# Zero rows on GpSimd's DMA queue, and ScalarE's work for a later half in four blocks: a recurrence with a mixture of experts on one core

## The chip, the cores and the metric

The kernel runs on one core of a Trainium2 chip. The metric is the time of one execution on the device in microseconds. Five engines with their own instruction queues work beside one another and meet at semaphores: TensorE (PE, matmuls and transposes), VectorE (DVE), ScalarE (ACT), GpSimd (POOL) and SyncE (SP), which here only issues transfers. Sixteen DMA engines do the moving.

## The reference, cut to what matters

The input x has 4 sequences of 1024 tokens with 256 channels. It is normalised over the channels to xn, and xn goes two ways.

- A recurrence over the 1024 time steps: for every sequence and channel a state of 16 numbers, `h = dA_t * h + dB_t * x_t`. The decay is `dA = exp(clamp(dt * A))` with `dt = clamp(softplus(xn @ Wdt.T + b))`, and `B = xn @ WB.T`, `C = xn @ WC.T`. After each step the state of each sequence is scaled down to a norm of 20 where it is above, so step t needs the norm of step t-1. The output of a step is `y = sum_n h * C + Dp * x`.
- A mixture of 8 experts with top 2 of 8 and 1280 slots each: every token is sent to its two experts' slots, each expert does `gelu(x @ c_fc) @ c_proj` on its slots, and the results come back with their weights.

The output is `x + s * silu(experts)`, where s is the recurrence's output.

## The kernel before

**Preparation.** Eight chunks of 128 tokens by 4 sequences are loaded, normalised by VectorE (`statistics`, `normalize`, lines 583 to 607), turned by TensorE (`turn`, line 1039) and evacuated by ScalarE (`turned`, line 803). SyncE stores each chunk three times: as rows (`xnd`, line 361), times Dp (`dx`, line 363) and turned (`xts`, line 366). Line 606 makes `dx` in one of two buffers, so it waits for the store two chunks earlier. Then VectorE works out the slot of each token (lines 671 to 711), and its first step follows.

**The zero rows.** The slots of the experts that get no token have to hold zeros. `clear(i)` writes 1024 of the 10240 rows of `xg`, 1 KB each, from a tile of zeros (lines 354 to 356). Eight of the ten stand in SyncE's queue ahead of the eight chunks' stores, two behind them. GpSimd scatters the tokens onto `xg` later (`send`, line 507), two steps apart from step 12 on, and before its first scatter it waits for all ten (line 545).

**The recurrence.** VectorE does 1024 steps, each with six operations (lines 722 to 755); GpSimd gives each step's scale (line 531) between lines 725 and 751. TensorE and ScalarE make what the steps need, four steps (a quad) at a time: TensorE transposes the decays (line 1176) and spreads the inputs with `pick` (line 1182), ScalarE copies the first to `da` (line 959) and scales the second to `ur` (line 966). Sixteen steps are a block, four blocks (64 steps) a half. VectorE waits for a quad's `ur` at line 736. ScalarE may be at most about two blocks ahead (line 946), TensorE waits for ScalarE's `ur` of the quad before (line 1178).

**Work for later halves.** For a half h, ahead of its time:
- TensorE's `time_rates(h, 6)` (line 1062) and ScalarE's `logs_of(h, 6)`: four copies out of PSUM (lines 817, 819), Exp (823) and Ln (824); then VectorE's `add_all_logs` (618) and ScalarE's `soft_clamp` (828).
- TensorE's `b_and_c` (1072) and ScalarE's `b_and_c_out` (836 to 838).
- ScalarE's `squares_of` (844), TensorE's `sums_of_squares` (1082, 1084) and ScalarE's `sums_out` (850).
- ScalarE's decays of the next half: 32 Tanh operations, two or three a quad (line 858), and at the end of a group of four blocks four exponentials over the whole half (`decay_ops`, line 870). TensorE waits for these before the next group's first transposes (line 1167).

All of the TensorE parts use PSUM bank 6, which the experts' row turns (line 1118) use as well; the tuple `waiting` names the last eviction of it that has to be done. Before, ScalarE does `logs_of` at the end of each group's fourth block, directly behind `decay_ops`; TensorE's `time_rates` is behind the fourth block's fourth quad.

**The experts' work** lies between the quads in a list fixed when the kernel is built: `by_quad` gives each quad up to three items, "up" (line 1194, eight matmuls, then a Gelu on ScalarE, line 974), "turn" (line 1118, then a copy, line 978) and "down" (line 1210, 16 matmuls a time, then a copy, line 985). It begins at quad 39, after all the scatters.

**ScalarE's functions** need a table each; where the next function isn't in the loaded ones, an ACT_TABLE_LOAD stands in the trace ahead of it.

Of the kernel before, what the change touches and what calls it, by code (L numbers as in the profile page):

```python
# [18 lines left out]
NB, NT, D, NS = 4, 1024, 256, 16  # L19
NE, CAP, FF = 8, 1280, 1024  # L20
P = 128
# [3 lines left out]
CH = NT // P  # L25
# [3 lines left out]
NBLK = NT // BLK  # L29
# [4 lines left out]
SLOTS = NE * CAP  # L34
# [10 lines left out]
HALVES = NT // HALF  # L45
# [6 lines left out]
def build(nc, x, wdtT, bdt, wb, wc, a_log, dpar, w_g, c_fc, c_proj, out):  # L52
# [4 lines left out]
    with ctx:  # L57
# [20 lines left out]
        zeros = sb("zeros", [P, 2 * D])  # L78
# [247 lines left out]
        delayed = sorted(k + 1 for k in at_step)  # L326
        sum_at, input_at, norm_at = {}, {}, {}
        for h in range(2, HALVES):
            for table, pieces, lo_, hi_ in ((sum_at, 1, 4 * h - 8, 4 * h - 6), (input_at, 2, 4 * h - 5, 4 * h - 3), (norm_at, 1, 4 * h - 2, 4 * h)):
                lo_, hi_ = max(lo_ * BLK + 3, BLK + 2), max(hi_ * BLK, 2 * BLK)  # L330
                free_ = [k for k in delayed if lo_ <= k < hi_ and k not in sum_at and k not in input_at and k not in norm_at]
                spare = [k for k in range(lo_, hi_) if k not in free_ and k not in sum_at and k not in input_at and k not in norm_at]
                chosen = sorted((free_ + spare)[:pieces])
                assert len(chosen) == pieces, (h, lo_, hi_)
                for c, k in enumerate(chosen):
                    table[k] = (h, c)
# [5 lines left out]
        def _(sp):  # L342
# [8 lines left out]
            for b in range(NB):  # L351
                sp.dma_start(dx[0:YPAD, b, :], zeros[0:YPAD, 0:D]).then_inc(padz, 16)

            def clear(i):
                sp.dma_start(xg[i * NT:(i + 1) * NT, :].rearrange("(r p) d -> p r d", p=P),
                             zeros[:, 0:D].unsqueeze(1).broadcast_to([P, CH, D])).then_inc(moe_zero, 16)

            for i in range(CH):
                clear(i)
                sp.wait_ge(xn_ready, i + 1)  # L360
                sp.dma_start(xnd.rearrange("(b i p) d -> p b i d", p=P, i=CH)[:, :, i, :], xnat[:, :, i, :]).then_inc(xn_out, 16)
                sp.wait_ge(dxn_ready, i + 1)
                sp.dma_start(dx_tok[:, i], dxn[:, i % 2]).then_inc(dx_done[i % 2], 16)
                if i >= 1:
                    sp.wait_ge(xt_sb, i + 1)
                    sp.dma_start(xts[i], xnT[:, i]).then_inc(xT_out, 16)
# [11 lines left out]
            sp.wait_ge(padz, 16 * (NB + 1))  # L378
            sp.sem_inc(y_out, 1)
            sp.dma_start(dxt, dx[0:BLK, :, :].rearrange("t b (k d) -> (t b k) d", k=DH)).then_inc(dx_in, 16)  # L380
            for i in range(CH, SLOTS // NT):
                clear(i)
            for k in range(2):
                sp.wait_ge(dx_done[k], 16 * CH // 2)
            sp.wait_ge(xn_out, 16 * CH)
# [74 lines left out]
        def _(pool):  # L460
# [42 lines left out]
            for i in range(CH):  # L503
                pool.wait_ge(stat_ready, i + 1)
                g.tensor_tensor(rs[:, :, i], vare[:, i, :], neghalf[:, :], ALU.pow).then_inc(rstd_ready, 1)

            def send(n):

                j, k = divmod(n, 2)
                first, home = homes[home_of(j)]  # L510
                g.indirect_dma_start(out=xg, out_offset=bass.IndirectOffsetOnAxis(ap=slot_of[:, k, j:j + 1], axis=0),  # L511
                                     in_=home[:, j - first, :], in_offset=None).then_inc(sent, 16)
# [27 lines left out]
            for step in range(NT):  # L540

                kind, n = at_step.get(step, ("", 0))
                if kind == "send":
                    if n == 0:
                        pool.wait_ge(moe_zero, 16 * (SLOTS // NT))
                    else:
                        pool.wait_ge(sent, 16 * n)
# [233 lines left out]
        def _(act):  # L781
# [161 lines left out]
            for blk in range(NBLK):  # L943
# [7 lines left out]
                for q in range(QPB):  # L951
# [38 lines left out]
                        weights_of(quad - COMBINE_AT)  # L990
                    if 0 <= quad - COMBINE_AT - 1 < 2 * CH:
                        gate_of(quad - COMBINE_AT - 1)
                    if blk % 4 == 0 and blk > 0 and q == 1 and blk // 4 + 2 < HALVES:
                        b_and_c_out(blk // 4 + 2, 6)
                    if blk % 4 == 1 and q == 0 and 2 <= blk // 4 + 1 < HALVES:
                        sums_out(blk // 4 + 1, 6)
                    if q == QPB - 1 and blk + 1 < NBLK:
                        inputs_out_of_psum(blk + 1)
# [14 lines left out]
                        decay_ops(1 - f).then_inc(decay_ready, 1)  # L1013
                    if q == 2 and blk < 3:
                        decay_op(0, blk + 1)
                    if blk == 0 and q == 1:
                        logs_of(2, 6)
                    if blk == 0 and q == 2:
                        b_and_c_out(2, 6)
                if blk % 4 == 3 and blk + 4 < NBLK:  # L1020
                    if (blk + 9) // 4 < HALVES:
                        logs_of((blk + 9) // 4, 6)
                if blk % 4 == 2 and blk // 4 + 2 < HALVES:
                    soft_clamp(blk // 4 + 2)
                if blk % 4 == 0 and 2 <= blk // 4 + 1 < HALVES:
                    squares_of(blk // 4 + 1)
            act.wait_ge(u_done, QUADS + 1)
            act.sem_inc(u_done, 1)
# [6 lines left out]
        def _(pe):  # L1035
# [126 lines left out]
            for blk in range(NBLK):  # L1162
# [5 lines left out]
                for q in range(QPB):  # L1168
# [43 lines left out]
                            last.then_inc(mm2_ps, 1)  # L1212
                    if 0 <= quad - COMBINE_AT < 2 * CH:
                        combine(quad - COMBINE_AT)
                    h = {(3, 3): blk // 4 + 3, (0, 1): blk // 4 + 2, (1, 0): blk // 4 + 1}.get((blk % 4, q), 0)
                    if blk == 0:
                        h = {1: 2, 2: 2}.get(q, 0)
                    if 2 <= h < HALVES:
                        if turns:
                            pe.wait_ge(xt_in, turns)  # L1220
                        after_evictions()
                        if blk % 4 == 3 or (blk == 0 and q == 1):
                            pe.wait_ge(xch_in[h // 2 % 2], 16 * ((h // 2 + 1) // 2))
                            time_rates(h, 6)
                            waiting = [z_used, h + 1]
                        elif blk % 4 == 0:
                            b_and_c(h, 6)
                            waiting = [bc_used, h + 1]
                        else:
# [48 lines left out]
```

## Time and profile before

| | |
|---|---|
| median of 3 runs | 1704.61 us (1703.8 to 1704.99) |
| the profiled execution | 1704.6 us, span 1702.6 us |
| VectorE busy | 1549.6 us (91%) |
| TensorE busy | 1291.1 us (76%), weight loads 1136.9 (67%) |
| ScalarE busy | 1225.1 us (72%) |
| GpSimd busy | 770.4 us (45%) |
| DMA | 113.29 MB, 67 GB/s in the mean; 332 and 340 GB/s in the first two fortieths |

The span falls into four stages: preparation (0 to 80 us), steps with the scatters beside them (to about 326), steps with the experts' matmuls (to about 1500), steps with the gathers and the end. Times in the rows are from the span's start. A row of waits names the instruction that waited, what released it, the sum in us, how often and the longest. Idle time before an instruction stands in brackets at the end of a row of the timeline, with what ended it. The engines' names in the rows are PE, ACT, DVE, POOL and SP; "q" behind one is its instruction queue.

### The profile page before, as it was taken

To read this page: it belongs to the slowest core of one execution; us is meant where nothing else is said; L and a number is where in the kernel's file an instruction comes from. 1 tells how busy PE (TensorE), PEld (TensorE's weight loads), DVE (VectorE), ACT (ScalarE), POOL (GpSimd) and SP (SyncE) were. 2 spreads that over 40 slices of the span, in tenths; PEclk is the share of its full clock that TensorE was granted. 3 is DMA by queue.
4 is the path that set the end of the run, shared out by engine and by line. 5 is a ranking of instruction groups with operands and counts; after the bars stand their busy time and mean duration, and the time that the engine had idled before them with its cause. 6 is when DMAs were issued, how large, how long until landed. Compare 5 with 4: busy or idle time off the path is not lost.

```text
span 1702.6 us, 33871 instructions
## 1 busy us (share of the span) xinstructions
PE 1291.1 (76%) x9356; PEld 1136.9 (67%) x9356; DVE 1549.6 (91%) x9454; ACT 1225.1 (72%) x3152; POOL 770.4 (45%) x1254
## 2 busy tenths in 40 slices
PE   5864435297979797997979798897979798855661
PEld 5753324286868686886868687796878687744551
DVE  6688888899999999998999899999989999987778
ACT  3697548278787887868787887878787777756451
POOL 3156666543434344343444344343434434468842
PEclk8576767698989899998989999898989899877785
DMA  9931111210111021021002002011101110012245
GB/s 332 340 127 47 44 41 44 95 36 17 51 49 46 17 77 31 18 62 50 28 24 86 24 26 75 25 39 37 63 18 34 66 32 20 20 44 71 75 127 202
DMA packets 95533, 113.29 MB, mean 67 GB/s; under 512 B 8432, under 2 KB 85360, under 8 KB 95344
## 3 DMA queue, kind: packets, MB, share of 16 engines
q1 hardware_dynamic: 87696, 94.13, 17.0%
q0 software_dynamic: 6144, 16.79, 3.1%
q8 instruction: 74, 1.21, 0.3%
q14 instruction: 115, 0.94, 0.2%
q10 hardware_dynamic: 1504, 0.22, 0.1%
HBM read 60.91 MB, written 50.20 MB: 65 GB/s over the span
## 4 chain that ended last, share of the span: by engine, by line
PE 54%; DVE 14%; ACT 12%; issue 7%; POOL 7%; DMA 4%; SPq 1%; POOLq 0%; ACTq 0%; DVEq 0%
PE ps L1210 15%; PE ps L1194 13%; PE ps L1182 10%; PE ps L1176 6%; ACT arena L870 4%; POOL arena L531 4%; DVE arena L751 3%; POOL xg L511 3%; PE ps L1141 3%; PE ps L1157 3%; DVE arena L722 2%; DVE arena L728 2%; DVE arena L740 2%; DVE arena L736 2%; ACT arena L858 2%
## 5 line engine op out<-in xcount | busy, mean ns | idle before, releaser
L531 POOL TENSOR_TENSOR arena<-arena,neghalf 128x1 f32<-128x1 f32 x1025 | 591.8, 577 | 851.2 <-DVE arena L725 780.3
L751 DVE SCALAR_TENSOR_TENSOR arena<-arena 128x128 f32<-128x128 f32 x1024 | 361.6, 353 | 54.0 <-POOL arena L531 53.6
L1182 PE MATMUL ps<-arena,pick 128*128 128x128 f32 x2048 | 301.9, 294 | 38.8 <-ACT arena L966 19.8
L736 DVE CUSTOM_DVE_ANT_0 arena<-arena 128x128 f32<-128x128 f32 x1024 | 294.0, 287 | 30.3 <-ACT arena L966 25.4
L1176 PE MATMUL ps<-ident,arena 128*128 128x128 f32 x1024 | 210.7, 333 | 137.6 <-ACT arena L870 132.0
L966 ACT ACTIVATE arena<-ps,arena 128x128 f32<-128x128 f32 x1024 | 291.4, 376 | 32.8 <-PE ps L1182 32.8
L1182 PEld LDWEIGHTS ps<-arena,pick 128*128 128x128 f32 x2048 | 280.2, 211 | 50.9 <-ACT arena L966 38.0
L1194 PE MATMUL ps<-arena,wf 128*128 128x256 f32 x1280 | 302.0, 386 | 8.1 <-issue 8.1
L728 DVE CUSTOM_DVE_ANT_0 arena<-arena 128x128 f32<-128x128 f32 x1024 | 299.0, 292 | 0.0
L1210 PE MATMUL ps<-wp,arena 128*128 128x256 f32 x1280 | 295.8, 385 | 2.6 <-ACT arena L974 2.3
L1176 PEld LDWEIGHTS ps<-ident,arena 128*128 128x128 f32 x1024 | 179.9, 244 | 167.4 <-ACT arena L870 137.2
L722 DVE TENSOR_TENSOR arena<-arena 128x128 f32<-128x128 f32 x1024 | 290.3, 283 | 0.0
L740 DVE TRANSPOSE_TENSOR_REDUCE arena<-arena 128x2 f32<-128x64 f32 x1024 | 251.3, 245 | 35.5
L858 ACT ACTIVATE arena<-arena,a16c,a 128x256 f32<-128x256 f32 x512 | 278.7, 610 | 0.1
L1194 PEld LDWEIGHTS ps<-arena,wf 128*128 128x128 f32 x1280 | 240.7, 195 | 38.9 <-issue 9.3
L1210 PEld LDWEIGHTS ps<-wp,arena 128*128 128x128 f32 x1280 | 241.7, 194 | 34.1 <-ACT arena L974 2.7
L755 DVE TENSOR_TENSOR_SCAN arena<-arena 128x2 f32<-128x2 f32 x1024 | 220.7, 215 | 0.0
L959 ACT ACTIVATE arena<-ps 128x512 f32<-128x512 f32 x256 | 151.9, 593 | 74.4 <-PE ps L1176 74.0
L725 DVE TENSOR_SCALAR arena<-arena 128x1 f32<-128x1 f32 x1024 | 149.3, 146 | 0.0
L974 ACT ACTIVATE arena<-ps 128x512 f32<-128x512 f32 x160 | 95.3, 607 | 62.5 <-PE ps L1194 59.9
L920 ACT ACTIVATE arena<-arena,winmask 128x16 f32<-128x16 f32 x520 | 110.9, 316 | 21.2 <-POOL arena L538 21.0
L1137 PE MATMUL ps<-arena,ident 128*128 128x128 f32 x132 | 32.6, 334 | 109.8 <-ACT arena L920 105.5
(146 smaller groups left out, 1379.7 us busy)
## 6 DMA issues: line engine op xcount, KB each, us to landing
xg<-zeros SPq DMA_DIRECT2D x10, 1024.0 KB, 9.6
xrow<-xg SPq DMA_DIRECT2D x40, 256.0 KB, 2.7
yg<-arena SPq DMA_DIRECT2D x40, 256.0 KB, 2.2
arena<-in_x SPq DMA_DIRECT2D x16, 512.0 KB, 9.3
wf<-in_c_fc SPq DMA_DIRECT2D x8, 1024.0 KB, 5.0
wp<-in_c_proj SPq DMA_DIRECT2D x8, 1024.0 KB, 6.0
arena<-dx SPq DMA_DIRECT2D x66, 64.0 KB, 2.4
ys<-arena SPq DMA_DIRECT2D x66, 64.0 KB
```

Source lines behind the costliest of these rows:

```text
L531: g.tensor_tensor(sv[:, slot, 1:2], mx, neghalf[:, 0:1], ALU.pow).then_inc(s_ready, 1)
L722: v.tensor_tensor(vv, hr[:, before, :], da[:, slot, :], ALU.mult).then_inc(v_ready, 1)
L728: v.tensor_tensor_reduce(out=junk[:, 0, :], in0=vv, in1=ur[:, slot, :], scale=2.0 / CLAMP ** 2, scalar=0.0, op0=ALU.mult, op1=ALU.add, acc ...
L736: v.tensor_tensor_reduce(out=junk[:, 1, :], in0=vv, in1=vv, scale=1.0 / CLAMP ** 2, scalar=0.0, op0=ALU.mult, op1=ALU.add, accum_out=ac[:, ...
L740: v.tensor_reduce(out=terms[:, slot, 0:2], in_=ac.unsqueeze(2).broadcast_to([P, 2, 32]), axis=AX.X, op=ALU.add, apply_transpose=True).then ...
L751: v.scalar_tensor_tensor(hr[:, slot, :], vv, sv[:, before, 1:2], ur[:, slot, :], ALU.mult, ALU.add)\
L858: last = a.activation(dst[:, :, k, n_, :], src[:, :, k, :], ACT.Tanh, scale=a16[:, c:c + 1], bias=a16c[:, c:c + 1])
L966: last = a.activation(ur[:, t + j, :], ps[2][:, j * P:(j + 1) * P], ACT.Copy, scale=terms[:, t + j, 3:4])
L1176: last = t.transpose(ps[q % 2][:, j * P:(j + 1) * P], tanhb[:, f, :, s], ident[:, :])
L1182: last = t.matmul(ps[2][:, j * P:(j + 1) * P], pick[:, q * QUAD + j, :], xin, start=True, stop=True)
L1194: last = t.matmul(ps[4 + j % 2][:, c * TS:(c + 1) * TS], wf[:, k, (2 * j + c) * P:(2 * j + c + 1) * P], xt[:, k, :], start=k == 0, stop=k ...
L1210: last = t.matmul(ps[7][:, j * D:(j + 1) * D], hid[:, k, j * P:(j + 1) * P], wp[:, k, :], start=k == 0, stop=k == FC - 1)
```

## The change

The ten transfers of zeros are issued by GpSimd, behind its last `rstd` and ahead of the clearing of `sv`, `hr` and `win`. Before its first scatter GpSimd also waits for `memz`. For halves from 2 on, `time_rates` and `logs_of` stand in the second quad of a group's first block, `b_and_c` and its copies in the second quad of the second block, `sums_of_squares` and its copy in the first quad of the third, `squares_of` at the end of the second. VectorE's `add_all_logs` comes 16 steps later (`sum_at`). `soft_clamp` and `decay_ops` stay.

```diff
-            for table, pieces, lo_, hi_ in ((sum_at, 1, 4 * h - 8, 4 * h - 6), (input_at, 2, 4 * h - 5, 4 * h - 3), (norm_at, 1, 4 * h - 2, 4 * h)):
+            for table, pieces, lo_, hi_ in ((sum_at, 1, 4 * h - 7, 4 * h - 5), (input_at, 2, 4 * h - 5, 4 * h - 3), (norm_at, 1, 4 * h - 2, 4 * h)):
...
-            def clear(i):
-                sp.dma_start(xg[i * NT:(i + 1) * NT, :].rearrange("(r p) d -> p r d", p=P),
-                             zeros[:, 0:D].unsqueeze(1).broadcast_to([P, CH, D])).then_inc(moe_zero, 16)
-
             for i in range(CH):
-                clear(i)
                 sp.wait_ge(xn_ready, i + 1)
...
-            for i in range(CH, SLOTS // NT):
-                clear(i)
...
+            for i in range(SLOTS // NT):
+                g.dma_start(xg[i * NT:(i + 1) * NT, :].rearrange("(r p) d -> p r d", p=P),
+                            zeros[:, 0:D].unsqueeze(1).broadcast_to([P, CH, D])).then_inc(moe_zero, 16)
+
             def send(n):
...
                     if n == 0:
+                        pool.wait_ge(memz, 1)
                         pool.wait_ge(moe_zero, 16 * (SLOTS // NT))
...
-                    if blk % 4 == 0 and blk > 0 and q == 1 and blk // 4 + 2 < HALVES:
+                    if blk % 4 == 1 and q == 1 and blk // 4 + 2 < HALVES:
                         b_and_c_out(blk // 4 + 2, 6)
-                    if blk % 4 == 1 and q == 0 and 2 <= blk // 4 + 1 < HALVES:
+                    if blk % 4 == 2 and q == 0 and 2 <= blk // 4 + 1 < HALVES:
                         sums_out(blk // 4 + 1, 6)
...
-                    if blk == 0 and q == 1:
-                        logs_of(2, 6)
-                    if blk == 0 and q == 2:
-                        b_and_c_out(2, 6)
-                if blk % 4 == 3 and blk + 4 < NBLK:
-                    if (blk + 9) // 4 < HALVES:
-                        logs_of((blk + 9) // 4, 6)
+                    if blk % 4 == 0 and q == 1 and blk // 4 + 2 < HALVES:
+                        logs_of(blk // 4 + 2, 6)
                 if blk % 4 == 2 and blk // 4 + 2 < HALVES:
                     soft_clamp(blk // 4 + 2)
-                if blk % 4 == 0 and 2 <= blk // 4 + 1 < HALVES:
+                if blk % 4 == 1 and 2 <= blk // 4 + 1 < HALVES:
                     squares_of(blk // 4 + 1)
...
-                    h = {(3, 3): blk // 4 + 3, (0, 1): blk // 4 + 2, (1, 0): blk // 4 + 1}.get((blk % 4, q), 0)
-                    if blk == 0:
-                        h = {1: 2, 2: 2}.get(q, 0)
+                    h = {(0, 1): blk // 4 + 2, (1, 1): blk // 4 + 2, (2, 0): blk // 4 + 1}.get((blk % 4, q), 0)
...
-                        if blk % 4 == 3 or (blk == 0 and q == 1):
+                        if blk % 4 == 0:
...
-                        elif blk % 4 == 0:
+                        elif blk % 4 == 1:
```

## Rows read from the trace of the kernel before

**Rows 1.** Page, costliest groups: operation, count, busy us, mean ns, idle before, releaser.
```profile
L736 DVE CUSTOM_DVE_ANT_0 arena<-arena 128x128 f32<-128x128 f32 x1024 | 294.0, 287 | 30.3 <-ACT arena L966 25.4
```

**Rows 2.** Busy us by engine (PE, PEld, DVE, ACT, POOL), granted clock, DMA, middle stage.
```profile
397.40:1450.40 1053.00, 923.97 (x6784) 820.64 (x6782) 1006.36 (x6362) 841.17 (x2144) 416.97 (x746) 0.95 0.13 41
```

**Rows 3.** Waits in the middle stage: VectorE's, TensorE's and ScalarE's longest.
```profile
DVE arena L736 <- ACT arena L966: 21.7, 10, 3.8
...
PE ps L1176 <- ACT arena L870: 89.9, 10, 9.0
...
ACT arena L985 <- PE ps L1210: 61.4, 27, 2.3
```

**Rows 4.** The same view as rows 2: the first and the last of eleven groups.
```profile
397.40:493.05 95.65, 85.73 (x627) 76.31 (x626) 92.96 (x590) 77.07 (x197) 38.63 (x69) 0.95 0.15 48
...
1360.69:1450.44 89.75, 79.03 (x600) 70.05 (x598) 86.30 (x546) 72.28 (x190) 35.68 (x64) 0.97 0.08 25
```

**Rows 5.** Timeline of TensorE around one group's decays (start us, us, operation, count).
```profile
671.18 1.91 PE L1062 MATMUL ps<-arena 128*128 128x256 f32 x8
...
682.19 1.15 PE L1176 MATMUL ps<-ident,arena 128*128 128x128 f32 x4 [8.99 <-ACT arena L870]
...
695.23 0.85 PE L1176 MATMUL ps<-ident,arena 128*128 128x128 f32 x4
695.92 1.06 PE L1182 MATMUL ps<-arena,pick 128*128 128x128 f32 x8
696.81 1.89 PE L1194 MATMUL ps<-arena,wf 128*128 128x256 f32 x8
698.54 0.60 PE L1118 MATMUL ps<-ident,xrow 128*128 128x128 f32 x4
```

**Rows 6.** Timeline of ScalarE around the same decays.
```profile
673.23 0.28 ACT L912 ACTIVATE arena<-ps 128x128 f32<-128x128 f32 x1 [1.25 <-PE ps L1124]
673.53 1.28 ACT L870 ACT_TABLE_LOAD   x1
...
682.04 0.46 ACT L817 ACTIVATE arena<-ps,arena 128x256 f32<-128x256 f32 x1
...
683.61 0.63 ACT L823 ACTIVATE arena<-arena 128x512 f32<-128x512 f32 x1
684.26 1.28 ACT L824 ACT_TABLE_LOAD   x1
685.56 0.63 ACT L824 ACTIVATE arena<-arena 128x512 f32<-128x512 f32 x1
...
686.21 1.70 ACT L920 ACTIVATE arena<-arena,winmask 128x16 f32<-128x16 f32 x8
687.80 0.57 ACT L959 ACTIVATE arena<-ps 128x512 f32<-128x512 f32 x1
688.27 1.11 ACT L966 ACTIVATE arena<-ps,arena 128x128 f32<-128x128 f32 x4
689.40 1.28 ACT L974 ACT_TABLE_LOAD   x1
```

**Rows 7.** The same view as rows 2: preparation and the steps before the first scatter.
```profile
0.00:72.00 72.00, 49.30 (x313) 45.50 (x314) 46.27 (x150) 40.67 (x79) 22.68 (x36) 0.70 1.01 345
72.00:98.00 26.00, 18.22 (x132) 14.95 (x131) 23.40 (x120) 17.90 (x43) 7.22 (x13) 0.63 0.87 282
```

**Rows 8.** Timeline of VectorE in the preparation.
```profile
25.76 1.23 DVE L606 TENSOR_TENSOR wf<-arena 128x1024 f32<-128x1024 f32 x1 [3.22 <-DMA dx<-wf]
...
65.35 0.42 DVE L675 COPY arena<-ps 128x256 f32<-128x256 f32 x1 [4.82 <-PE ps L1054]
```

**Rows 9.** Timeline of GpSimd: the first scale and the first scatter.
```profile
80.94 0.59 POOL L531 TENSOR_TENSOR arena<-arena,neghalf 128x1 f32<-128x1 f32 x1 [26.29 <-DVE arena L725]
...
99.99 1.24 POOL L511 DMA_INDIRECT xg<-wf,slot_of  x1 [0.23 <-issue]
```

**Rows 10.** The zero rows' issues on SyncE: duration in ns, min/median/max.
```profile
L355 SPq DMA_DIRECT2D xg<-zeros x10: 434/1233/1668, 15.7 to 75.7; - x10
```

## The prediction

> **What bounds the kernel now.** I read the page's costliest groups first. VectorE carries the recurrence, 1024 steps of six operations, and hardly ever stops: in the whole run 25.4 us stand before line 736, where it waits for ScalarE's `ur` [rows 1]. The edits of ScalarE's order can win these at most. Next I cut the span by stage. In the middle stage (397 to 1450 us: eleven groups of 64 steps, the expert matmuls beside them) VectorE is busy 1006 of 1053 us, TensorE 924, ScalarE 841 [rows 2]. Busy shares don't say who leads, so I read the waits of that stretch. TensorE waits 89.9 us for the decay exponentials (line 870), about 9.0 in each group. ScalarE waits for TensorE; its longest row is 61.4 us, and no row of it in this stretch names VectorE. VectorE waits 21.7 us for ScalarE [rows 3]. So TensorE and ScalarE run freely at TensorE's pace and VectorE catches up with them once per group. A group takes 95.65 us (first of eleven) to 89.75 us (last), 95.7 in the mean, (1450.44 - 397.40) / 11 [rows 4]. TensorE's ledger for these 1053 us is 924 of work, 90 at the decays and the rest small. VectorE alone would need (1053 - 21.7) / 11 = 93.8. What makes TensorE's order longer makes the kernel longer, one for one; what shortens it pays only down to 93.8, about 21 us in all.
>
> **ScalarE's lump, taken apart.** Before, ScalarE runs the four decay exponentials at the end of a group's fourth block and the logs of a later half directly behind them. TensorE has the half's time-rate matmuls behind it by then: 8 matmuls of 1.9 us before it stops for 8.99 us [rows 5]. The logs fall beside TensorE's first matmuls of the next group: from 682.19 on, that engine shows no wait, although ScalarE makes the four evacuations, Exp, a table load and Ln from 682.04 to 686.1 [rows 5, 6]. They are covered.
> The change moves the time rates and the logs to the second quad of the next group's first block, and B and C, the sums and the squares by one block each. What follows:
> - At the decays the 1.9 us of time rates go, so the last transpose comes earlier, and with it the copy of line 912, which waited 1.25 us for it here [rows 6]. The decays start 1.3 us earlier in this group, up to 2 in others, and TensorE's stop of 9.0 stays, since it is the decays' own length.
> - The same 1.9 us now stand among TensorE's other work. Together: 0 to +0.6 us per group.
> - The logs lose their cover. I walk the group after the lump at 682, where the third quad holds one "up" (8 matmuls) and a "turn", and the fourth a "down". After the time rates TensorE has left, until it needs ScalarE's next `ur` (the picks of the fourth quad): four transposes 0.69, eight picks 0.89, the up 1.73, the turn 0.5, four transposes 0.69, in all 4.5 us (start to start) [rows 5]. ScalarE in that time: four evacuations 1.57, a table load 1.28, Exp 0.65, a load 1.30, Ln 0.63, then `da` 0.47 and `ur` 1.11 of the third quad, 7.0 us [rows 6]. TensorE stops for 2.5. Then ScalarE needs another load (1.28) and 0.6 for the Gelu that the down waits for, while TensorE has 0.9 of picks: another 1.0. Cost here 3.5 us.
> - The load before Exp is new. After a Gelu the resident tables lack Exp (a load stands before the decays too, at 673.53 [rows 6]), and now a Gelu mostly comes between decays and logs. Where the logs stood right behind the decays, Exp follows with no load [rows 6].
> - Gained: the window copies (from 686.21) come earlier and TensorE's output matmuls no longer wait for them, 0.5 us a group at most.
> I walked both engines' orders through all eleven groups with these durations. For the order before this gives 95.9 us per group (the trace: 95.7), for the new order 99.2: between -0.5 and +4.9 by group, because a group whose first quads hold only "down" keeps its tables and has more to do. Eleven groups: +36. Without the new load before Exp the same walk gives 2.2 per group, +25; with all table loads at nothing, +10; below, where TensorE could always fill the gap, the 21 us that VectorE waits could go. I take +31, between the first two, because the loads' row is plain and their number is not. Once, 2 us come back: `ur` of a group's first quad is 5 us earlier, but VectorE then meets the third quad's, which is later. Lump: +29.
> The row for tables is the load of 1.28 us that stands before the first Gelu after Ln [rows 6]. The Trainium skill (ScalarE: Activation LUTs, "Table sets: the hidden batching unit") speaks against this move: calls are to be batched by table set, not by function, and the logs' Exp and the decays' Exp were such a batch. By its figure of 2.7 us for a switch, two more a group would be 59 us of ScalarE; by the row they are 28, and only what TensorE cannot fill counts.
> The soft clamp's and the norms' waits stay met: ScalarE is at most two blocks ahead, and VectorE's additions for a half, now 16 steps later, are still more than a block before their readers. No cost.
>
> **The zero rows.** Ten transfers of 1 MB (1024 rows of 1 KB each) leave SyncE's queue, where issuing one took 1.23 us in the median [rows 10]. What goes is their share of the transfers beside the preparation: in 0 to 72 us the DMA engines are full (share 1.01, 345 GB/s) [rows 7]. VectorE waits there for the stores of `dx`, 3.22 us at 25.76 being the first of five. But the routing, which leads to the first step, starts at 65.35 after 4.82 us of waiting for TensorE's logits [rows 8]; so only part of a faster VectorE arrives. Bounds 0 and 8; I take 2, as ScalarE's logs and TensorE's queue of logits stand right behind the first of these waits.
> What comes: ten issues in GpSimd's queue before it clears `hr`, `sv` and `win`, and VectorE's first step waits for that. GpSimd stands idle for 26.3 us before its first scale at 80.94 [rows 9], so the issues are hidden up to 2.6 us each. The trace has no such issue. Nearest rows: the same transfer on SyncE, 1.23 us, and GpSimd's scatter of 128 rows, 1.24 us [rows 9, 10]. If the price goes by rows it is 8 x 1.24 = 9.9 us. The same regular transfer is the nearer row, as the scatter must read an index for each row; I take up to 2.5, so nothing, and keep 9.9 for the range.
> The clears must land before the first scatter. Before, 72 x 345 + 26 x 282 GB/s = 32 MB were moved by 98 us [rows 7], just before the first scatter at 99.99 [rows 9]. Now the first 50 us hold only loads and stores, 4.5 MB of inputs and zeros and six chunks of 1.57 MB, so 14 MB. The other 18 MB need 53 us at 345 GB/s and end at 103. The scatter's turn would be at 98. If the row loads end last, no wait; if the clears do, 5 us. I take 3. Zero rows together: -2 + 3 = +1, from -8 to +5.
> The DMA engines were full whoever issued. The Trainium skill (DMA: Bandwidth & Descriptors, "Issuing engines are not separate DMA queues") says that transfers from all three queues share the same engines and another queue saves issue time alone; the share of 1.01 agrees, and by it this part is worth nothing. The same page ("Anatomy of one DMA — SWDGE (gpsimd) path") calls descriptor generation small; by that the ten issues hide. No run here shows it.
>
> **Sum.** The profiled execution took 1704.6 us (span 1702.6 and 2.0 around it), the median of the runs is 1704.61, so nothing is to be converted. 1704.6 + 29 + 1 = 1734.6, said as 1735.
>
> **Rivals.**
> - *GpSimd's issue goes by rows.* For it: an engine that works in software, and 1.24 us for only 128 rows. Against: the scatter's price may be mostly fixed. From 2.6 us each it delays the first step by ten times the excess: at 4 us 14, at 9.9 us 73. Time 1735 to 1808, about 1750 likeliest.
> - *VectorE's waits simply go* (the other side). At the lump the first `ur` comes 5 us earlier, and VectorE's longest wait there is 3.8 [rows 3]. If TensorE fills the logs' window by itself, its group falls below 93.8 and all 21 go: 1704.6 - 21 - 1 = 1683. It decides when the new stops are under about 0.5 us per group. Against: TensorE has almost no idle time but the decays.
> - *Nothing moves.* New stops just equal what is gained at lump and windows: 1702 to 1708.
>
> **Chances.** Forecast 0.53 (its own range 1714 to 1748), issue by rows 0.30, waits go 0.11, nothing moves 0.06. This kernel's runs can tell 0.2%, 3.4 us. Faster 0.11, same 0.06, slower 0.83. The range leaves out the first rival's far end and the faster case: 1705 to 1778.
>
> **What would show it.** GpSimd: ten direct issues, each under 2.6 us, and VectorE's first step at 78 to 80; later means the first rival. The first scatter at 98 to 103. In the middle stage: groups of 98 to 100 us; TensorE idle for ScalarE's `ur` (line 1182) in the first block; table loads before the logs' Exp; VectorE's wait at line 736 near 50 us, moved from the first quad to the third. Groups of 94 us, or no TensorE stop after the time rates, make the forecast wrong.

## The result and the profile after

The changed kernel takes 1761.97 us (1759.46 to 1762.54, 4 runs), beside 1704.8 us for the kernel before on the same chip: a ratio of 1.0331, 95% interval 1.0313 to 1.0349. It is 57 us slower, where 30 were forecast. The direction and the mechanism of the lump held; the size did not. The time lies inside the stated range of 1705 to 1778, but 14 us above the forecast's own part of it, 1714 to 1748. The room above that was kept for GpSimd's issue going by rows, which did not happen. That the range held was therefore luck. The profiled execution took 1762.5 us (span 1760.5), so its rows can be compared with those of before directly.

First the page: the costliest groups (as rows 1) and the zero rows' line of the DMA issues. Line numbers are 2 to 7 lower than before: L734 was L736, L1175 was L1182, L868 was L870.
```profile
L1175 PE MATMUL ps<-arena,pick 128*128 128x128 f32 x2048 | 309.9, 300 | 74.7 <-ACT arena L964 46.2
L734 DVE CUSTOM_DVE_ANT_0 arena<-arena 128x128 f32<-128x128 f32 x1024 | 294.6, 288 | 79.3 <-ACT arena L964 49.7
...
xg<-zeros POOLq DMA_DIRECT2D x10, 1024.0 KB, 23.2
```
VectorE's wait for `ur` (L734 for L964) rose from 25.4 us [rows 1] to 49.7. A piece of zero rows lands 23.2 us after its issue in the median. The trace has 71 table loads where the kernel before has 51: nine more ahead of the logs' Exp (L821), nine ahead of a Gelu (L972) and two ahead of a Tanh (L856).

The stages, as rows 2 and 7: preparation, the steps before the first scatter of the kernel before, and the eleven groups.
```profile
0.00:72.00 72.00, 47.92 (x317) 43.26 (x317) 48.02 (x154) 40.67 (x79) 31.60 (x46) 0.73 0.88 298
72.00:98.00 26.00, 7.57 (x57) 6.63 (x58) 8.22 (x29) 3.98 (x11) 1.43 (x3) 0.51 1.03 345
403.97:1511.12 1107.15, 942.04 (x6806) 836.12 (x6806) 1019.37 (x6420) 874.61 (x2171) 423.89 (x753) 0.94 0.13 39
```
The second row is new: from 72 to 98 us, VectorE is busy 8.22 us, where it was 23.40 [rows 7], with the DMA engines full.

The third row runs from one group's first ScalarE copy (L947, line 949 before) to that of the group eleven later, as [rows 2] does, and gives 1107.15 / 11 = 100.65 us a group. It can't be set beside the 95.7 of [rows 4]: before, the logs stand ahead of that copy where the row begins and no more where it ends, and now they stand ahead of it at neither end. VectorE's steps have no such shift. Line 736 (now 734) in steps 184 and 888, counted from 0, which lie eleven groups apart, before and after:
```profile
391.61 0.28 DVE L736 CUSTOM_DVE_ANT_0 arena<-arena 128x128 f32<-128x128 f32 x1
...
1447.82 0.28 DVE L736 CUSTOM_DVE_ANT_0 arena<-arena 128x128 f32<-128x128 f32 x1
```
```profile
403.65 0.28 DVE L734 CUSTOM_DVE_ANT_0 arena<-arena 128x128 f32<-128x128 f32 x1
...
1504.33 0.29 DVE L734 CUSTOM_DVE_ANT_0 arena<-arena 128x128 f32<-128x128 f32 x1
```
A group took 1056.21 / 11 = 96.02 us and takes 1100.68 / 11 = 100.06: 4.0 us more, 44.5 in the eleven. Another 12.0 us are lost ahead of step 184.

The waits of the eleven groups, VectorE's and then TensorE's, as rows 3.
```profile
DVE arena L734 <- ACT arena L964: 47.1, 19, 6.1
DVE arena L734 <- PE ps L1134: 16.0, 12, 3.5
```
```profile
PE ps L1169 <- ACT arena L868: 103.9, 11, 9.9
PE ps L1175 <- ACT arena L964: 20.9, 13, 4.4
PE ps L1175 <- ACT arena L910: 18.9, 26, 3.0
```
TensorE stops for `ur` (L1175 for L964) 13 times, 20.9 us, and 18.9 us for the copies of line 910. The stop at the decays nearly keeps its length: 9.4 us in the mean of eleven, where it was 9.0 [rows 3].

One new stop from close by: the group that begins at 1000 us, TensorE first and then ScalarE.
```profile
1012.46 1.91 PE L1055 MATMUL ps<-arena 128*128 128x256 f32 x8
...
1017.81 0.75 PE L1169 MATMUL ps<-ident,arena 128*128 128x128 f32 x4
1021.43 1.16 PE L1175 MATMUL ps<-arena,pick 128*128 128x128 f32 x8 [2.87 <-ACT arena L964]
1023.34 6.78 PE L1203 MATMUL ps<-wp,arena 128*128 128x256 f32 x16 [0.75 <-ACT arena L972]
```
```profile
1014.40 0.47 ACT L815 ACTIVATE arena<-ps,arena 128x256 f32<-128x256 f32 x1 [0.16 <-PE ps L1055]
...
1015.99 1.28 ACT L821 ACT_TABLE_LOAD   x1
...
1017.94 1.28 ACT L822 ACT_TABLE_LOAD   x1
...
1020.25 1.13 ACT L964 ACTIVATE arena<-ps,arena 128x128 f32<-128x128 f32 x4
1021.40 1.28 ACT L972 ACT_TABLE_LOAD   x1
```
This is the walk of the prediction: the time rates (at 1012.46), two quads, then TensorE waits 2.87 us, while ScalarE makes evacuations, a load, Exp, a load and Ln. Here the evacuations start as the time rates end, and `ur` is through at 1021.4. A third load (L972) delays the Gelu for which the "down" at 1023.34 waits 0.75 us. The walk had 2.5 and 1.0.

What it did not have stands in the last row of TensorE: the 16 matmuls of the down take 6.78 us, where such a down takes 3.62 at a granted clock of 1.00 (at 667.73 us in the kernel before). The granted clock of these microseconds (the column before the last two):
```profile
1019.00:1022.00 3.00, 0.57 (x5) 0.57 (x6) 0.55 (x4) 2.97 (x8) 0.00 (x0) 1.00 0.34 109
1022.00:1025.00 3.00, 2.25 (x10) 1.79 (x9) 2.93 (x19) 2.99 (x6) 1.17 (x2) 0.62 0.00 0
1025.00:1028.00 3.00, 3.00 (x8) 2.37 (x8) 2.93 (x20) 1.26 (x5) 1.17 (x2) 0.50 0.00 0
1031.00:1034.00 3.00, 3.00 (x19) 2.74 (x18) 1.98 (x14) 3.00 (x14) 1.17 (x2) 1.00 0.01 3
```
The clock was still 1.00 in the stretch of the stop itself. It fell behind the stop, to 0.50, which is 1.2 GHz of 2.4, and was 1.00 again in the stretch from 1031 us on.

### The profile page after: what moved, and what is told of

The parts are those of the page before. It is cut to its first block, busy times and chain, and to the rows that moved or that the text cites. A ratio compares the mean times of both kernels' runs of the same rounds, so it can differ in the third digit from the quotient of the medians.

```text
span 1760.5 us, 33893 instructions
## 1 busy us (share of the span) xinstructions
PE 1300.3 (74%) x9356; PEld 1145.4 (65%) x9356; DVE 1554.2 (88%) x9454; ACT 1254.7 (71%) x3172; POOL 781.9 (44%) x1264
## 3 DMA queue, kind: packets, MB, share of 16 engines
q1 hardware_dynamic: 77296, 83.64, 14.7%
## 4 chain that ended last, share of the span: by engine, by line
PE 54%; ACT 17%; DVE 9%; POOL 7%; issue 7%; DMA 5%; SPq 0%; POOLq 0%; ACTq 0%; DVEq 0%
PE ps L1203 15%; PE ps L1187 14%; PE ps L1175 10%; PE ps L1169 6%; ACT arena L868 4%; POOL arena L528 4%; PE ps L1134 3%; POOL xg L508 3%; PE ps L1150 3%; DVE arena L749 2%; ACT arena L856 2%; ACT arena L964 2%; DMA xts<-arena 1%; DVE arena L720 1%; PE ps L1055 1%
## 5 line engine op out<-in xcount | busy, mean ns | idle before, releaser
L1175 PE MATMUL ps<-arena,pick 128*128 128x128 f32 x2048 | 309.9, 300 | 74.7 <-ACT arena L964 46.2
L734 DVE CUSTOM_DVE_ANT_0 arena<-arena 128x128 f32<-128x128 f32 x1024 | 294.6, 288 | 79.3 <-ACT arena L964 49.7
L1175 PEld LDWEIGHTS ps<-arena,pick 128*128 128x128 f32 x2048 | 286.5, 215 | 88.7 <-ACT arena L964 69.3
L964 ACT ACTIVATE arena<-ps,arena 128x128 f32<-128x128 f32 x1024 | 291.5, 375 | 42.0 <-PE ps L1175 40.6
L1187 PE MATMUL ps<-arena,wf 128*128 128x256 f32 x1280 | 307.2, 391 | 8.9 <-issue 7.4
L856 ACT ACTIVATE arena<-arena,a16c,a 128x256 f32<-128x256 f32 x512 | 278.6, 609 | 0.1
L1187 PEld LDWEIGHTS ps<-arena,wf 128*128 128x128 f32 x1280 | 244.8, 198 | 41.5 <-issue 8.6
L972 ACT ACTIVATE arena<-ps 128x512 f32<-128x512 f32 x160 | 94.9, 604 | 67.0 <-PE ps L1187 64.7
L868 ACT ACTIVATE arena<-arena 128x2048 f32<-128x2048 f32 x60 | 109.8, 1910 | 0.1
## 6 DMA issues: line engine op xcount, KB each, us to landing
xg<-zeros POOLq DMA_DIRECT2D x10, 1024.0 KB, 23.2
```

The costliest lines, as they stand in the source:

```text
L734: v.tensor_tensor_reduce(out=junk[:, 1, :], in0=vv, in1=vv, scale=1.0 / CLAMP ** 2, scalar=0.0, op0=ALU.mult, op1=ALU.add, accum_out=ac[:, ...
L856: last = a.activation(dst[:, :, k, n_, :], src[:, :, k, :], ACT.Tanh, scale=a16[:, c:c + 1], bias=a16c[:, c:c + 1])
L964: last = a.activation(ur[:, t + j, :], ps[2][:, j * P:(j + 1) * P], ACT.Copy, scale=terms[:, t + j, 3:4])
L1175: last = t.matmul(ps[2][:, j * P:(j + 1) * P], pick[:, q * QUAD + j, :], xin, start=True, stop=True)
L1187: last = t.matmul(ps[4 + j % 2][:, c * TS:(c + 1) * TS], wf[:, k, (2 * j + c) * P:(2 * j + c + 1) * P], xt[:, k, :], start=k == 0, stop=k ...
```

## The experiments

Every run is a ratio to the kernel before on the same chip. "Group" is an eleventh of the time from VectorE's step 184 to its step 888 in the profiled execution (96.02 before).

| run | median us | ratio, 95% interval | group us |
|---|---|---|---|
| e1_zero_rows_only | 1720.86 | 1.0082 [1.0057, 1.0106] | 96.19 |
| e2_order_only | 1751.60 | 1.0260 [1.0237, 1.0284] | 100.13 |
| e3_order_no_tables | 1712.60 | 1.0034 [1.0025, 1.0044] | 96.69 |
| e4_small_parts_only | 1715.45 | 1.0054 [1.0035, 1.0072] | 96.99 |
| e5_zero_rows_spread | 1711.69 | 1.0038 [1.0028, 1.0048] | 96.22 |
| e6_rates_in_long_stop | 1684.88 | 0.9878 [0.9853, 0.9902] | 94.54 |
| e8_before_no_log_tables | 1693.05 | 0.9927 [0.9900, 0.9955] | 95.28 |
| e9_one_load_fewer | 1740.52 | 1.0201 [1.0175, 1.0228] | 99.08 |
| e10_stop_and_one_set | 1679.93 | 0.9843 [0.9827, 0.9860] | 94.25 |
| e12_last_two_behind_dx | 1708.46 | 1.0018 [1.0009, 1.0028] | 96.05 |
| e13_busy_in_stop | 1687.56 | 0.9890 [0.9873, 0.9906] | 94.41 |
| e14_busy_in_new_stop | 1751.42 | 1.0260 [1.0243, 1.0277] | 100.09 |

The kernel before had medians of 1706.79 (e1 to e4), 1705.53 (e5 to e9), 1705.11 (e10 to e13) and 1706.87 (e14).

**The two halves of the change apart.** e1 is the zero rows' hunks of the diff alone, e2 the rest alone.

> The zero rows on GpSimd's queue, ScalarE's and TensorE's order as before. Theory: the ten issues are cheap (9 us in all), but their 10 MB reach the DMA engines in one piece at 46 to 55 us and the turned chunk and the first dx load, which the first steps need, queue beside them; the second step starts 12 to 15 us later and nothing gives it back: 1715 to 1719 us. Rival: the late start of the changed kernel came from its order in the first block, then 1702 to 1706 here.

> The order of the changed kernel, the zero rows on SyncE's queue as before. Theory: TensorE stops for ScalarE's ur behind the uncovered logs; the groups of the middle stage take about 100 us instead of 95.7, the start is as before: 1745 to 1752 us. Rival (both changes only cost together, because a late start takes ScalarE's lead away): 1715 to 1735.

+14 and +45, together 59, beside the 57 of both: the parts add up. e2 lies in its theory's range. e1 lies 1.9 us above its own and far from its rival.

**The lump's parts.** e3 is e2 with other functions in the later halves' logs; e4 moves B and C, the sums and the squares and leaves logs and time rates where they were.
```
e3: - a.activation(flat, flat, ACT.Exp, scale=-1.0)       + ... ACT.Exp if h < 2 else ACT.Tanh ...
    - a.activation(flat, flat, ACT.Ln, bias=1.0)          + ... ACT.Ln if h < 2 else ACT.Tanh ...
e4: - h = {(3, 3): blk//4 + 3, (0, 1): blk//4 + 2, (1, 0): blk//4 + 1}
    + h = {(3, 3): blk//4 + 3, (1, 1): blk//4 + 2, (2, 0): blk//4 + 1}   (ScalarE's readers moved alike)
```


> As the order alone, but the Exp and Ln of the later halves' logs are Tanh, which leaves the softplus out and needs no table load. Theory: the loads are about half of what the order costs, since they lengthen the stretch in which TensorE waits, and the logs' own 3 us stay uncovered: 1722 to 1732 us. Rival, the loads are all of it: 1703 to 1710. Rival, the loads are hidden and the place alone costs: above 1740.

> Logs and time rates stay behind the decays as before; only B and C, squares and sums go one block later each, zero rows on SyncE. Theory: these parts are covered at either place, 1702 to 1708 us. Rival, the small parts delay the input copy of a block (TensorE's wait for line 910 doubled in the changed kernel) and carry a good part of the loss: 1712 to 1725.

Both of my theories missed. e3 has 40 table loads fewer than e2 (31 for 71, counted in the traces) and is 39 us shorter, so a load costs nearly its whole length in the new order. The old order pays for loads too, so this is not yet their share of the order's 45 us; e8 below gives it. And the small parts, which I had at no cost, take 8.7 us alone. TensorE's waits of the eleven groups in e4:
```profile
PE ps L1135 <- ACT arena L920: 7.7, 9, 2.9
...
PE ps L1080 <- ACT arena L978: 5.3, 2, 3.3
```
Line 1080 (the sums of squares) now waits in its new block for the copy of a row turn (line 978), which uses the same bank 6, 3.3 us at once, a row that the same view of the kernel before does not have; L1135, the output's first matmul, waits 7.7 us where it waited 5.7. VectorE's wait for `ur` in the same stretch rises from 21.7 [rows 3] to 26.9 us, and 4.6 us for the output come beside it. The time is the rival's, but its mechanism is not: TensorE's wait for line 912 stays at 9.3 us in e4. It is 19.0 in e2 and 10.1 in e3, so it doubles with the loads.

**What a load costs in either place.** e8 is the kernel before with e3's edit; e9 is e2 with one load for Exp and Ln together.
```
e9: + if h >= 2: a.preload_act_table_set("natural_log_exp_and_others")     (ahead of the logs' Exp)
```


> Control for the run of the new order without table loads: the order before, with Tanh in place of Exp and Ln in the later halves' logs, which leaves the softplus of those halves out and with it two table loads per half. Theory (in the order before the loads lie in the stretch that ScalarE has to itself beside TensorE's long stop, and cost little): 1697 to 1706, so that the 39 us that the same edit took off the new order are the new place's. Rival (a load costs wherever it stands, 11 halves by 2 to 3 loads of 1.28 us and the eviction behind them): 1665 to 1690.

> The new order alone (zero rows as before, measured 1751.6), with the table set that holds both Exp and Ln loaded ahead of a later half's logs, so that Exp and Ln need one load between them and not two. Theory (each load there is on the path and is followed by the stop and the lower clock): 12 loads of 1.28 us fewer, 1.3 to 2.5 us each with what follows: 1722 to 1740. Rival (the wait for the logs is already covered, only the whole stop's going helps): 1745 to 1753.

e8 lies between theory and rival: 20 loads fewer gave 12.5 us, 0.6 each, so the old place was not free of cost either. e9 came 0.5 us above its theory's range, with nine loads fewer, not twelve. In the new place 40 gave 39 us (e3) and 9 gave 11 (e9): 1.0 to 1.2 us each, about the whole 1.28 us of a load. e3 and e8 are the same edit in the two orders. It takes 39.0 us off the new one and 12.5 off the old, so 26.5 of the order's 45 us come from the loads, nearer to e3's theory (about half) than to its rival (all). The other 18 come with the order without them, the small parts' among these.

**Where the 9-us stop could be used.** e6 leaves the lump where it was and takes the time rates into TensorE's stop; e10 adds to it one table set for decays and logs; e13 does e6's time rates five times over.
```
e6:  - h = {(3, 3): blk//4 + 3, (0, 1): ...}          (ahead of the fourth block's last quad)
     + turn_inputs(...); time_rates(blk//4 + 3, 6)    (behind the block, before the wait for the decays)
e10: + a.preload_act_table_set("natural_log_exp_and_others")     (ahead of the decays)
e13: - time_rates(h, 6)                               + time_rates(h, 6, 5)
```


> The kernel before with the time rates (16 matmuls of 64 columns) of a later half taken from their place ahead of the group's fourth block's last quad into TensorE's 9-us stop at the end of that block, where TensorE waits for ScalarE's decays; ScalarE's lump stays where it was. Theory (TensorE's order sets the length of a group and the 9 us are empty): about 1.6 us less per group, 11 groups, 1684 to 1697. Rival (the logs now start later behind the same decays, so that the order of the next block is later by as much): 1702 to 1712.

> The kernel with the time rates in TensorE's 9-us stop (measured 1684.9), and in it the table set that holds Exp and Ln loaded ahead of the decays, so that the logs behind them need no load of their own. Theory (a load right behind the stop is on the path: the control without the logs' loads in the order before gained 12.5 us): 11 loads of 1.28 us fewer, 0.7 to 1.3 us each: 1669 to 1678. Rival (TensorE at the lower clock sets the end of that stretch, not ScalarE): 1681 to 1688.

> The kernel with the time rates in TensorE's 9-us stop (measured 1684.9), with those matmuls done five times over into the same bank with the same values, so that TensorE works through most of the stop instead of resting: more work, nothing else. Theory (TensorE comes out of a rest of this kind at the lower granted clock and pays for it in the next 5 to 6 us): the granted clock stays at 1.00 behind the stop, the four downs and ups there take 3.6 us in place of 5 to 7, and a group is 0.5 to 2 us shorter: 1662 to 1680. Rival (VectorE or ScalarE sets that stretch, the clock is beside the path): 1683 to 1690. Rival (the repeats delay the logs or the next block): 1690 or more.

e6 is as the theory said: 20.6 us faster than before, 1.2%, with the same work. TensorE and VectorE in the eleven groups of e6:
```profile
PE ps L1176 <- ACT arena L870: 74.2, 10, 7.6
```
```profile
DVE arena L736 <- ACT arena L966: 6.0, 7, 2.1
```
TensorE waits 74.2 us for the decays in ten stops of the eleven groups, where it waited 89.9 [rows 3]: each stop shrank by the 1.6 us that now stand in it. VectorE's wait fell from 21.7 us [rows 3] to 6.0, by as much. e10, at 1679.93, is the best version found, 1.6% under the kernel before, though it came out between theory and rival, 5 us under e6 with overlapping intervals. The two profiled executions lie 8 us apart (each is the slowest of its four): 3.0 us ahead of step 184, 3.2 in the eleven groups, the rest behind. Eleven loads fewer in the groups gave 0.3 us each, so behind the stop a load is mostly hidden. VectorE's waits at line 736 are down to 3.2 us in e10's eleven groups; there is little left to gain from this order.

e13 asks what the low clock behind a stop costs. TensorE around the decays in e13:
```profile
666.91 8.88 PE L1062 MATMUL ps<-arena 128*128 128x256 f32 x40
676.45 0.85 PE L1176 MATMUL ps<-ident,arena 128*128 128x128 f32 x4 [0.66 <-ACT arena L870]
...
678.03 1.89 PE L1194 MATMUL ps<-arena,wf 128*128 128x256 f32 x8
682.22 0.49 PE L1137 MATMUL ps<-arena,ident 128*128 128x128 f32 x2 [2.30 <-ACT arena L920]
```
The repeats fill the stop (0.66 us left) and the eight matmuls of the up take 1.89 us at full clock, where e6 has 2.53. But the next matmuls then wait 2.30 us for ScalarE's window copies (L920), over the eleven groups 18.7 us where e6 has 5.1. The time is e6's within 3 us, in the first rival's range. But VectorE waits only 6.0 us for `ur` in e6's eleven groups, so its own steps fill nearly all of a group, and no more than those 6 us were left to win there. The run shows only that the low clock behind the long stop is not what holds e6 back. It does not separate ScalarE's window copies from VectorE's own steps as the reason.

**The same question in the new stop.** e14 is e2 with the transposes of one quad done three times over.
```
e14: - for j in range(QUAD):   + for j in list(range(QUAD)) * (3 if blk % 4 == 0 and q == 2 and ... else 1):
```


> The new order alone (measured 1751.6), with the four transposes of the quad at which TensorE then waits for ScalarE's logs done three times over into the same bank, so that TensorE works through about 1.5 us of its new stop of 2.9 to 4.4 us instead of resting: more work, nothing else. Theory (behind that stop the downs and ups take 4.6 to 6.8 us in place of 3.6, at the lower granted clock, and that is on the path, about 1 us per group): the clock stays at 1.00 behind most stops, 1733 to 1744. Rival (as in the long stop of the order before, the lower clock is beside the path): 1747 to 1754. Rival (the repeats hold up the quad's products, which come out of the same transposes): 1755 or more.

The time fell into the first rival's band, but the run does not decide. The repeats came a quad too early:
```profile
1000.45 1.88 PE L1171 MATMUL ps<-ident,arena 128*128 128x128 f32 x12
...
1007.70 1.16 PE L1177 MATMUL ps<-arena,pick 128*128 128x128 f32 x8 [1.71 <-ACT arena L966]
1009.61 6.77 PE L1205 MATMUL ps<-wp,arena 128*128 128x256 f32 x16 [0.75 <-ACT arena L974]
```
The stop was shorter by 1.1 us, and the down behind it still took 6.77 us. So it shows only that 1.1 us more of TensorE's work ahead of the stop costs nothing, because ScalarE sets when it ends. What the low clock behind the new stops adds stays open.

**The zero rows.** e5 sends them on GpSimd's queue too, but one piece behind each of the eight powers; e12 also holds the last two back.
```
e5:    g.tensor_tensor(rs[:, :, i], vare[:, i, :], neghalf[:, :], ALU.pow)
     + clear(i)                                       (pieces 8 and 9 behind the loop)
e12: + pool.wait_ge(dx_in, 16); clear(8); clear(9)    (behind the clearing of win)
```


> The kernel before with the ten pieces of zero rows on GpSimd's queue, but spread: one piece behind the power of each of the eight chunks of normalisation, the last two behind the eighth, where SyncE had them nearly so. Theory (the 13 to 14 us of the start come from 10 MB lying in one piece before the first turned chunk's store and the first load of dx): the start is as in the kernel before (step 0's scan within 3 us, first scatter within 5 us), 1701 to 1712. Rival (another queue's packets slow SyncE's transfers however they are spread, or GpSimd's issue holds up the powers): step 0 is 8 us late or more, 1713 to 1725. Rival (every issue between two powers delays the normalisation by its 0.9 us): 1710 to 1714.

> The spread zero rows on GpSimd's queue (measured 1711.7), with the last two of the ten pieces held back until the first load of dx has landed, as they lay behind it on SyncE's queue in the kernel before. Theory (what counts is the bytes that the 16 DMA engines have to move ahead of the first load of dx: 2 MB at 345 KB per us are 6 us): 1702 to 1707, start within 2 us of the kernel before. Rival (the queue itself, or the slower normalisation beside its issues, costs the 6 us): 1709 to 1713.

The loss went from 14 us to 6 and then to 3 (ratio 1.0018). Neither theory held whole. e5's time lies in the ranges of its theory and of its last rival, but its step 0 came 7.2 us late, where the theory allowed 3. e12 came 1.5 us above its theory's range and just under its rival's, with step 0 5.5 us late. The transfers say more. e12's load of `dx`:
```profile
74.59 0.35 SPq L375 DMA_DIRECT2D arena<-dx  x1
```
It leaves at 74.59 us, where it left at 74.86, and has landed by 78.35, when GpSimd issues the last two pieces behind it; before, it landed at 78.41. So the order of the bytes held this load up in e1, not the queue. What is left stands in e12's VectorE:
```profile
33.19 1.22 DVE L609 TENSOR_TENSOR wf<-arena 128x1024 f32<-128x1024 f32 x1 [10.43 <-DMA dx<-wf]
...
53.32 1.38 DVE L600 TENSOR_SCALAR arena<-arena,mv,rstd 128x256 f32<-128x256 f32 x4
...
56.80 4.22 DVE L600 TENSOR_SCALAR arena<-arena,mv,rstd 128x256 f32<-128x256 f32 x4
...
71.07 0.42 DVE L678 COPY arena<-ps 128x256 f32<-128x256 f32 x1 [6.58 <-PE ps L1057]
```
GpSimd's first four pieces are issued at 10 to 23 us, the moment each power is done, where SyncE's first four left at 16 to 32. They now stand beside the first chunks' stores, and VectorE waits 10.4 us for the store of `dx` at 33.19. The routing starts at 71.07, not 65.35 [rows 8], and the first step follows it without a wait.

## Why the prediction was right or wrong

**The lump: right mechanism, two terms too small.** The logs lose their cover, TensorE stops, a load before Exp is new: all there. VectorE's wait moved as forecast, too: about 37 of its 47 us in the eleven groups now stand ahead of a third quad. My walk gave +36 with all loads, +25 without the one before Exp, +10 without any. With the small parts' 8.7 us taken off (as if they simply added, which no run shows), the runs say 45 - 9 = 36 (e2) and 35 - 9 = 26 (e9). For the third, e3 gives 6 - 9 = -3 against the kernel before, and 18 - 9 = 9 against the order before without those loads (e8); the prediction does not say from which of the two its +10 counts. The walk was good; I did not believe it. The step that failed is "I take +31, between the first two": nothing in the rows spoke for the middle. No run isolates the 2 us that were to come back. "They are covered", of the logs in the old place, was not quite so: e8 gained 0.6 us for each load that it dropped there. The other failed step is "The soft clamp's and the norms' waits stay met ... No cost": I looked at VectorE's additions only. What came late was TensorE, where `b_and_c` and the sums meet other evacuations in ScalarE's queue (e4), +8.7.

The Trainium skill (ScalarE: Activation LUTs, "Table sets: the hidden batching unit") had the right warning, to batch calls by table set. Its 2.7 us for a switch is twice the 1.28 us of every load here, and the trace has only some 0.02 us of idle time beside one; the runs put the price in this place at 1.0 to 1.2 us each.

**The zero rows: +14 where I had +1.** The gain was there and worth nothing: the routing's scan came at 71.85 us, not 74.45, but VectorE then stood still. SyncE, VectorE and GpSimd after the change:
```profile
58.62 0.32 SPq L361 DMA_DIRECT2D xts<-arena  x1
82.68 0.32 SPq L364 DMA_DIRECT2D arena<-xts  x1
83.12 1.17 SPq L375 DMA_DIRECT2D arena<-dx  x1
```
```profile
71.85 1.22 DVE L697 TENSOR_TENSOR_SCAN wp<-wp 128x512 f32<-128x512 f32 x1
...
87.00 0.29 DVE L720 TENSOR_TENSOR arena<-arena 128x128 f32<-128x128 f32 x1 [9.02 <-issue]
...
95.97 0.30 DVE L734 CUSTOM_DVE_ANT_0 arena<-arena 128x128 f32<-128x128 f32 x1 [8.35 <-PE ps L1134]
```
```profile
46.37 9.14 POOL L501 DMA_DIRECT2D xg<-zeros  x10
...
87.44 0.62 POOL L528 TENSOR_TENSOR arena<-arena,neghalf 128x1 f32<-128x1 f32 x1 [27.54 <-DVE arena L723]
...
114.03 1.18 POOL L508 DMA_INDIRECT xg<-wf,slot_of  x1 [0.19 <-issue]
```
The ten issues took 9.14 us, 0.91 each, hidden as forecast; the first rival (issue by rows) fell. VectorE's first step, at 87.00, came later than 80 us, which the prediction would have read as that rival. That sign was wrong, as the step waited for something else. The first scatter, at 114.03, waited for nothing but its own late step, so the 3 us for the clears did not come either. GpSimd's first scale came at 87.44, not 80.94 [rows 9], because VectorE's first step did. What I left out was a wait of SyncE: the load of the first turned inputs (L364) waits until the last store of `xts`, issued at 58.62, has landed, which is at 82.7, 24.0 us later (7.6 before); and the first load of `dx` stands behind it. VectorE's first step waits 9.02 us, and line 734 of the same step another 8.35 for the output's matmuls, which need that `dx`. The bytes fit. Two stretches of the preparation, before and after:
```profile
26.00:46.00 20.00, 17.96 (x152) 16.90 (x152) 15.67 (x52) 11.87 (x26) 3.75 (x3) 0.58 1.05 379
46.00:72.00 26.00, 21.57 (x119) 19.97 (x120) 16.18 (x47) 20.79 (x40) 5.67 (x4) 0.50 1.04 364
```
```profile
26.00:46.00 20.00, 17.93 (x166) 16.76 (x165) 18.50 (x66) 12.74 (x29) 4.43 (x4) 0.67 0.72 271
46.00:72.00 26.00, 20.30 (x109) 17.97 (x109) 14.12 (x35) 20.03 (x38) 13.90 (x14) 0.50 0.93 312
```
Without pieces between the chunks, the DMA engines idle part of the time (share 0.72 and 0.93): 20 x (379 - 271) + 26 x (364 - 312) = 3500 KB are missing by 72 us. And two pieces, 2.1 MB, which SyncE issued behind that load of `dx`, lie ahead of it now. 5.6 MB at 345 GB/s are 16 us, as an estimate; the scan that ends VectorE's first step came 14.7 us late (96.7, not 82.0). The count is a rough one: only seven of the ten pieces had landed when the store of `xts` had, and the load of `dx` then took 10.0 us beside the last three, where it took 3.6 before. The failed step is "The clears must land before the first scatter": I counted the bytes ahead of the scatter, the last reader, and not those ahead of the first load.

The Trainium skill (DMA: Bandwidth & Descriptors, "Issuing engines are not separate DMA queues") says that all queues share the same engines; the trace agrees, as that store on SyncE's queue took 24 us beside GpSimd's pieces. I had read from it that the move is worth nothing. Sharing the engines is just what made it cost.

**The sum.** The two parts alone measured 59 us, I had 30. Of the 29 between, 13 are the zero rows' bytes, 9 the small parts, and 7 the distrust of my own walk (5) with the 2 us that I took off. "VectorE's waits simply go" fell with VectorE's wait at 47.1 us and groups of 100.06; I had forecast near 50 and 98 to 100. (That rival's sum takes the zero rows' +1 off instead of adding it: 1685, not 1683.) The floor of 93.8 us a group held in all runs: the shortest mean is e10's, 94.25.

## What to carry to other kernels

- Moving transfers to another queue changes their order against everything on the first queue. Count the bytes ahead of each load that the path waits for, the earliest first, not only ahead of the last reader.
- A batch of activations behind another of the same table set saves loads, and in this kernel a load cost 0.6 us there and 1.0 to 1.2 where the next engine waited for it; and an engine's long stop is a place for work that is ready (e6: the same work, 1.2% faster).
- When a walk through both engines' orders reproduces the trace of before, take its number for after, as would have served here.

## What the runs showed that was not expected

- GpSimd's issues of a 1 MB transfer with 1 KB rows cost 0.91 us each, SyncE's 0.43 to 1.67 [rows 10]. SyncE's 1.23 in the median was no fixed price: its store of `xts` took 1.24 us to issue in the middle of the preparation before, and 0.32 at 58.62 in the changed kernel. The DMA queues of the first 130 us (packets, MB, share) show that GpSimd's queue makes fewer and larger packets; before, SyncE's queue had 26848 packets for 32.71 MB and GpSimd's 384:
```profile
q1 hardware_dynamic: 16160, 22.09, 49.1%
q0 software_dynamic: 2912, 11.01, 25.6%
```
10.0 MB more in 2528 packets more, about 4 KB each, while SyncE's queue loses 10688 packets.
- In e12 the normalisation of the last chunk took 4.22 us where the others took 1.38 (the last one took 1.97 in the kernel before), beside a clearing of 4096 columns on GpSimd from 55.59 to 59.13 us. It is part of what e12 has left to lose; that the clearing is the reason was not tested. In the changed kernel that clearing stands behind the normalisation.
- The granted clock fell to 1.2 GHz behind the stop of 2.87 us in the changed kernel and behind the one of 2.30 us in e13 (0.63 in the mean from 682 to 685 us), and stayed there for several microseconds of work.
